# Waits for landed scatters on GpSimd between the attention steps and the expert blocks

## The reference, cut to what matters

```python
x = x + layernorm(linear_attention(layernorm(x)))       # x: 16 sequences of 256 tokens, 128 features, f32
x = x + layernorm(moe(layernorm(x)))

def linear_attention(x):                                 # 16 heads of 8 features, causal running sums
    q, k, v = split(x @ W_qkv + b_qkv)
    q, k = elu(q * 8 ** -0.5) + 1.0001, elu(k) + 1.0001
    return (q . cumsum(k v) / (q . cumsum(k) + 1e-6)) @ W_out + b_out

def moe(x):                                              # 4096 tokens, 8 experts, hidden size 512
    shared = gelu(x @ Wfc_s + bfc_s) @ Wproj_s + bproj_s
    gate = the two largest of softmax(x @ Wr), scaled to sum 1, else 0
    return shared + sum over e of gate[:, e] * (gelu(x @ Wfc[e] + bfc[e]) @ Wproj[e] + bproj[e])
```

## Time and profile before

| | |
|---|---|
| median of 3 runs | 392.34 us (391.49 to 393.35) |
| profiled execution, its own time | 392.23 us |
| its span | 390.4 us |
| granted TensorE clock, mean | 0.965 of full speed |
| TensorE, VectorE, ScalarE, GpSimd busy | 336.3, 287.0, 257.3, 266.9 us |
| scatters into the lists, into the results | 64, 78 |

### The profile page before, as it was taken

One profiled execution on the slowest core, in us unless ns is written; L12 is line 12 of the kernel. 1 busy time (PEld: TensorE's weight loads), 2 busy tenths in 40 slices (PEclk: granted clock), 3 DMA queues, 4 the chain that ended last, 5 costly groups with the idle time before them and its releaser, 6 DMA issues.

```text
span 390.4 us, 8117 instructions
## 1 busy us (share of the span) xinstructions
PE 336.3 (86%) x2497; PEld 293.4 (75%) x2497; DVE 287.0 (74%) x687; ACT 257.3 (66%) x692; POOL 266.9 (68%) x335
## 2 busy tenths in 40 slices
PE   6858797999998989987997665799998999989892
PEld 2537485886967868686796664799998999989871
DVE  4999997999899898999743260574544557777667
ACT  4977875887978869865365452446646676678674
POOL 8779696698687887878685737455564555866640
PEclk9999998999999999999998969599999999999998
DMA  7578558582755244160392435598787779988417
GB/s 201 158 220 211 135 160 134 141 215 66 211 141 162 64 120 117 56 182 29 110 319 93 123 105 153 157 249 275 227 260 241 211 272 362 299 264 258 133 49 203
DMA packets 53521, 69.17 MB, mean 177 GB/s; under 512 B 6365, under 2 KB 37386, under 8 KB 53482
## 3 DMA queue, kind: packets, MB, share of 16 engines
q1 hardware_dynamic: 47556, 58.58, 53.2%
q0 software_dynamic: 4544, 9.35, 6.9%
q10 hardware_dynamic: 1382, 0.79, 0.7%
HBM read 40.06 MB, written 18.15 MB: 149 GB/s over the span
## 4 chain that ended last, share of the span: by engine, by line
PE 29%; ACT 12%; another core or an unknown queue 9%; DVE 7%; POOL 7%; issue 7%; DVEq 0%; ACTq 0%; POOLq 0%
PE bS L1531 6%; PE bO L1531 5%; ACT hs L1134 4%; PE bO L1315 3%; POOL expert_lists L692 2%; PE bV L1504 2%; PE bV L1506 2%; PE bV L1505 2%; ACT hs L1005 1%; POOL Z L772 1%; ACT rows L861 1%; PE bA L1504 1%; POOL Z L779 1%; POOL Z L777 1%
## 5 line engine op out<-in xcount | busy, mean ns | idle before, releaser
L813 POOL DMA_INDIRECT expert_results<-yb,yrow x78 | 79.4, 1018 | 60.6 <-DVE yb L2135 37.1
L692 POOL DMA_INDIRECT expert_lists<-rows,pos x64 | 64.4, 1006 | 21.9 <-issue 19.9
L1682 DVE TENSOR_TENSOR_SCAN KV<-bS,KV 128x1024 f32<-128x1024 bf16 x32 | 72.8, 2278 | 0.3
L1315 PEld LDWEIGHTS bO<-wout_rot,Z 128*128 128x128 f32 x512 | 60.3, 192 | 11.2 <-POOL Z L772 6.7
L1315 PE MATMUL bO<-wout_rot,Z 128*128 128x128 f32 x512 | 63.4, 278 | 4.9 <-POOL Z L772 2.7
L2127 DVE COPY yrow<-xb 128x2 int32<-128x2 int32 x24 | 4.1, 169 | 45.6 <-remote 21.4
L1531 PE MATMUL bO<-KV,hs 128*128 128x128 f32 x232 | 30.5, 286 | 1.4 <-ACT hs L1134 1.4
L1531 PEld LDWEIGHTS bO<-KV,hs 128*128 128x128 f32 x232 | 28.9, 201 | 1.8 <-ACT hs L1134 1.8
L1134 ACT ACTIVATE hs<-bV,KV 128x256 f32<-128x256 f32 x56 | 22.0, 480 | 12.4 <-PE bV L1506 10.4
L1134 ACT ACTIVATE hs<-bA,Z 128x256 f32<-128x256 f32 x24 | 10.1, 471 | 29.1 <-remote 23.4
L1285 PE MATMUL bA<-w2s_sb,hs 128*128 128x128 f32 x224 | 28.8, 277 | 0.0
(11 more groups left out here) (368 smaller groups left out, 979.5 us busy)
## 6 DMA issues: line engine op xcount, KB each, us to landing
KV<-packed_weights SPq DMA_DIRECT2D x21, 578.0 KB
Z<-packed_weights SPq DMA_DIRECT2D x18, 578.0 KB
xb<-expert_lists SPq DMA_DIRECT2D x39, 129.0 KB
vr<-vr SPq DMA_DIRECT2D x16, 224.0 KB, 2.5
shared<-expert_results SPq DMA_DIRECT2D x7, 512.0 KB
vr<-vr SPq DMA_DIRECT2D x16, 192.0 KB
vr<-vr SPq DMA_DIRECT2D x16, 160.0 KB
vr<-vr SPq DMA_DIRECT2D x16, 128.0 KB
```

Source lines behind the costliest of these rows:

```text
L692: g.indirect_dma_start(out=lists, out_offset=bass.IndirectOffsetOnAxis(ap=pos[:, m:m + 1], axis=0), in_=rows[:, m // TILES, m % TILES, :], ...
L813: g.indirect_dma_start(out=results, out_offset=bass.IndirectOffsetOnAxis(ap=yrow[n][:, c], axis=0), in_=yb[n][:, c, :], in_offset=None).th ...
L1315: ins = t.matmul(bO[:, j * D:(j + 1) * D], Z[:, d, j * P:(j + 1) * P], wout_rot[:, d], start=False, stop=True, skip_group_check=True)
L1682: v.tensor_tensor_scan(w, ps_keep, w, 0.0, ALU.mult, ALU.add).then_inc(s["kv_sum"], 1)
```

## The change

Two places in GpSimd's program get waits. In `scatters`, from the last four scatters of set 5 on (`in_pairs`), GpSimd waits after every second scatter of a call until this one and all before it in its set have landed. In `scatter_block`, for blocks 0 to 11 (`PAIRED = 2 * NBUF`), it waits after the two scatters of a block until they have landed. In the calls for set 6 the first scatter stands alone, the other seven are 2 + 2 + 2 + 1, the last without a wait.

```diff
             AT_END = 4
+            PAIRED = 2 * NBUF
+
+            def in_pairs(i, first):
+
+                return i >= NS or (i == NS - 1 and first >= AT_END)

             def scatters(i, first, last):
...
                     g.indirect_dma_start(
                         out=lists, out_offset=bass.IndirectOffsetOnAxis(ap=pos[:, m:m + 1], axis=0),
                         in_=rows[:, m // TILES, m % TILES, :], in_offset=None).then_inc(landed, 16)
+                    if in_pairs(i, first) and (m - first) % 2 == 1:
+                        pool.wait_ge(landed, 16 * (m + 1 + (2 * TILES if i > NS else 0)))
...
                         out=results,
                         out_offset=bass.IndirectOffsetOnAxis(ap=yrow[n][:, c], axis=0),
                         in_=yb[n][:, c, :], in_offset=None).then_inc(blk_scat[n], 16)
+                if b < PAIRED:
+                    pool.wait_ge(blk_scat[n], 32 * turn(0) + 32)
```

## The result

The changed kernel takes 433.65 us (median of four runs, 431.46 to 435.25) where the kernel before takes 392.61 (four runs): a ratio of 1.1008 [1.0961 to 1.1055]. The forecast was 398 with 386 to 408 around it. It had the sign, and 5.5 of the 41 us.

What follows compares the result with a forecast made beforehand. TensorE was taken as the bound, busy 336.3 of 390.4 us. GpSimd's queue gave -5.0 us at the idle price, landings beside loads added 10.5: 392.2 + 5.5 = 397.7, rounded to 398, range 386 to 408.

Steps and rivals of the forecast that it cites:

- The reading of the runs: Between attention and expert blocks, long unbroken scatter runs go with late signals, ending 1.4 to 2 us after the run.
- Both pieces: Chain waits without known releaser, 8.75 us from 217.01 and 11.88 us from 234.24, should be gone.
- Rival 4: Late signals between attention and blocks come from something other than scatter runs; 398 to 400 us, within the forecast's chance.
- The chain of who waits for whom: In the expert blocks, block k's landing gates result k + 6, which gates the second layer of k + 8.
- The price of a wait up to block 2: On GpSimd's queue, 1.84 us per wait with idle DMA engines, plus half a load per two waits.
- half a load per two waits: Extra landing delay beside loads for the waits not among the nine tied ones, 2.8 us in all.
- The period of the tied pairs: After block 2, landings release loads that delay later landings: 0.85 us extra for nine waits, about 5.2 us per pair.
- Rival 2: Landings in blocks 2 to 11 delayed 2 us each; block 11 near 320, time 407 to 414; chance 0.12.
- The way from the landing to TensorE: From block 11's landing to block 19's second layer: 0.6 us, one write of 0.42 us and two signals.
- break-even: The change neither gains nor loses when block 11 lands at 302.2 us.
- From block 12 on GpSimd holds nobody: With no added waits there, GpSimd needs 2.5 us per block against 3.64 of the engines.
- Rival 1: Landings undelayed, 0 to 0.1 us extra per wait, stalls go; block 11 at 297 to 299, time 387 to 389; chance 0.31.

Runs made afterwards that it cites:

- held kernel: Kernel before, with GpSimd held in front of block 14's scatters until block 19's result is written: 407.01, 408.58 and 405.68 us (1.0257, 1.0308, 1.0279).
- spaced kernel: Changed kernel with every wait replaced by a rest, one small GpSimd operation of about 1 us: 395.12 us, 0.9964 of the kernel before.
- the mix: Kernel before plus small GpSimd operations after list pairs, blocks 0 to 5 and every second to 23, set 7 spread over blocks 2 to 5: 0.9728; 1.0371 elsewhere.

## Why the prediction was wrong, by its own steps

**The reading of the runs held.** Both pieces are gone, TensorE is busy in both stretches, and block 7's result comes 12.4 us earlier. The copy of the logits started at 223.44, within 0.1 us of the end of TensorE's logits (222.45 and 0.96 us), where it had been 5.5 us behind. It came only 2.3 us earlier than before because the logits themselves ended 3.1 us later: the norm's operations on GpSimd began at 214.03, before at 211.08, and not near 212.7. As forecast, this held nobody up. Rival 4 (the stalls don't come from the runs) falls with the held kernel on three chips of this kind. The "ten scatters in a row" up to 224.38 are nine by the trace, seven of set 6 and two of block 0. What the earlier trace rows could not show is that the effect belongs to some chips only.

**The chain of who waits for whom held.** Block 2 gates 8, block 11 gates 17, 17 gates 19. VectorE stood for landings ahead of blocks 8 to 17 (and of 7 and 18), and block 8's write was held until 272, not 258. TensorE was busy for 57% of the time from 245 to 305, where about 70% was forecast.

**The price of a wait up to block 2 was too low: +10.4.** By its own terms the prediction has block 2's scatters start at 201.7 + 24 x 1.27 + 1.8 + 11 x (1.84 + 0.23) = 256.8; they started at 267.21. The eleven gaps there sum to 36.2 us, where 11 x 2.14 (1.84 and the ordinary gap) are 23.5: 12.7 extra, with 2.6 forecast. Four gaps carry nearly all of it, 4.32, 4.01, 7.68 and 4.98. The cheapest, 1.58, 1.66 and 1.73, are below the idle price of 2.14. The mistake was to share out "half a load per two waits" evenly. The dearest two stand behind the results of blocks 0 and 1, and in that time SyncE issues a load of weights about every 3.8 us:

```profile
226.27 0.34 SPq L479 DMA_DIRECT2D KV<-packed_weights  x1
...
241.17 0.35 SPq L479 DMA_DIRECT2D Z<-packed_weights  x1
245.20 0.35 SPq L479 DMA_DIRECT2D KV<-packed_weights  x1
267.35 0.35 SPq L479 DMA_DIRECT2D KV<-packed_weights  x1
```

These are six loads from 226.27 to 245.20, and none after that for 22 us. The DMA engines' share is 0.99 from 240 to 245 (it was 0.16). Block 1's two scatters were issued from 242.43 and 243.69. From 242 to 244 the scatters' queue (q0) moved nothing; from 244 to 246 and from 246 to 248 it moved:

```profile
q0 software_dynamic: 7, 0.02, 3.1%
...
q0 software_dynamic: 55, 0.10, 15.7%
```

The change caused this: with the stall gone VectorE frees six buffers in a row, and the loads that follow stand beside the landings that GpSimd now waits for. That they hold them up is read from this timing; no run moved the loads alone. The prediction read the quiet DMA of the kernel before as the state of the changed one.

The quiet after it is the change's doing too, and the prediction had no term for it. Ahead of the load of block 13, SyncE waits until all of set 7 has landed (line 463). In the kernel before, it did not have to stand there at all; now this wait took (total, times, longest):

```profile
SPq L463 <- DMA expert_lists<-rows,pos: 19.3, 1, 19.3
```

It cost nothing here, since VectorE stood for block 2 anyway, and in that quiet time the last three of set 7's four waits were cheap (gaps of 1.66, 1.58 and 2.20 us).

**The period of the tied pairs was nearly right: +5.0.** From 267.21 to 317.96 there are nine pairs, 5.64 us each, where 5.2 was forecast. To the landing of block 11 it comes to 55.9 us against 50.9. Block 11 thus landed just ahead of 323.2 and not at 307.7. Rival 2 had this landing near 320, by another split: its 2 us extra at each of the ten blocks was too dear (measured 1.3), and it missed the four gaps.

**The way from the landing to TensorE was taken too short: +2.8.** The prediction gave it 0.6 us. The result of 17 is written at 323.21 and the second layer of 19 starts at 326.48, 3.3 us later. Between them stand VectorE's splits for block 20 (until 324.91) and block 20's whole first layer on TensorE. VectorE is in order: what stood behind its wait had to be done after it. So the break-even was near 299.5, not 302.2. These three and the 5.5 forecast make 23.7.

**"From block 12 on GpSimd holds nobody" failed: +12.7, and +1.6 ahead of it.** As a sum of rates it is true, 2.5 us per block against 3.64. But the landing of block 12 held VectorE once more for 3.51 us (the 1.6 above). And GpSimd was behind by eight blocks when its waits ended, and it caught up in one run of 16 scatters, just the pattern that the earlier trace rows had shown beside a stalled TensorE. The prediction looked for runs before block 12 only. The spaced kernel showed this by itself: with the waits gone and the rests ended at the same block, 9.92 us of the same kind came back.

Rival 1 (landings undelayed, 387 to 389) was given 0.31 and is what the round-robin rule of the Trainium skill ("DMA: Bandwidth & Descriptors", Queues, rings and completion order) would give, since by it a scatter passes beside a load. The gap of 7.68 us beside dense loads speaks against it once more.

**Left open.** The spaced and the held kernel show that the stall follows a run; the run of 16 was not broken in the changed kernel on a chip with the stall. The changed kernel itself was not timed on a chip of the second kind; with rests behind its waits it is 18% slower there. What holds TensorE during a run, and what differs between the chips, no row shows. It wasn't tried to take rows or descriptors out of the scatters to see whether the issue or the data does it, and set 7's spread alone was not run on a chip with the stall.

## What to carry to other kernels

A wait for a landed transfer on an in-order queue is priced by what that transfer will share the DMA engines with after the change, and it is paid by whoever's buffers are freed further down that queue. Where a change slows a queue for a stretch, look at how its backlog goes out when the stretch ends. Where a pattern of instructions must be broken up, a small operation between them or a spread of the work does it without waiting, and it is worth timing on more than one chip: the mix that gained 2.7% on one lost 3.7% on another.

## What the hardware showed that was not expected

Scatters of 128 rows issued by GpSimd every 1.27 us, nine or more without a break, went on three of five chips with a TensorE that did one matmul per 0.7 to 1.4 us (gaps of 1.14 and 1.04 us that nothing ended, in the rows at 338.00 and 341.51) and whose signals mostly came late too, in pieces of 7 to 14 us of the chain. Runs of four or five went with pieces of 2.2 to 6.1 us, the longest beside the run of five near 202 to 209 us in every kernel that kept it on these chips. The queues that load code moved nothing meanwhile, in the two runs shown above. On the other two chips runs of 43 showed none of it, and the kernel before took 363.9 us there against 393.7 to 396.7, about 8% less for the same program.

The gap in front of a pair ranged from 1.58 us with quiet DMA engines to 7.68 us beside loads, a factor of nearly five for the same wait.
